# Embedding bags, counted and gathered: 19 features counted and 13 gathered for 20 and 12, with a half round of row buffers behind GpSimd's loop

## What is computed

```python
emb = flat[ids + offs]                                   # (512, 32, 20, 64)
mask = (jnp.arange(L_) < lengths[..., None]).astype(emb.dtype)
pooled = jnp.einsum('bfle,bfl->bfe', emb, mask)
out = pooled.reshape(Bq, F_ * E_)                        # (512, 2048)
return jnp.nan_to_num(out)
```

## Time and profile before

| | |
|---|---|
| median of 3 runs | 1046.8 us |
| the profiled execution | 1047.35 us |
| its span, first to last instruction | 1045.4 us |
| TensorE matmul busy | 983.3 us, 94% |
| TensorE weight load busy | 864.1 us, 83% |
| VectorE busy | 937.4 us, 90% |
| ScalarE busy | 754.1 us, 72% |
| GpSimd busy | 666.0 us, 64% |
| mean share of the 16 DMA engines | about 40% |
| TensorE's granted clock, mean | 0.997 |

### The profile page before, as it was taken

The page is one execution under the profiler, slowest core; times in us unless marked ns, Lnnn a source line. Parts: engine busy times, 40 slices in busy tenths (PEclk is TensorE's granted clock), DMA queues, the critical chain, the costliest instruction groups (busy, mean ns, idle before and its releaser), DMA issues.

```text
span 1045.4 us, 29010 instructions
## 1 busy us (share of the span) xinstructions
PE 983.3 (94%) x9885; PEld 864.1 (83%) x9885; DVE 937.4 (90%) x2485; ACT 754.1 (72%) x1121; POOL 666.0 (64%) x617
## 2 busy tenths in 40 slices
PE   3499999999999999999999999999999999999996
PEld 0188888888888888888888888888888888888885
DVE  9987879898999989999989998999999898999980
ACT  2477777878686868787777777787868686877770
POOL 3874677676676756777667767767676775773010
PEclk9999999999999999999999999999999999999998
DMA  6234142534444343535252626244443434241300
GB/s 220 82 136 118 37 141 67 152 111 131 128 120 135 115 141 105 161 86 179 69 171 76 188 59 191 75 148 119 129 133 115 146 106 116 76 115 50 106 28 6
DMA packets 66140, 119.85 MB, mean 115 GB/s; under 512 B 31600, under 2 KB 33351, under 8 KB 66065
## 3 DMA queue, kind: packets, MB, share of 16 engines
q1 hardware_dynamic: 45696, 100.66, 30.0%
q0 software_dynamic: 19168, 17.93, 8.5%
q10 hardware_dynamic: 1200, 0.58, 0.2%
HBM read 83.45 MB, written 4.71 MB: 84 GB/s over the span
## 4 chain that ended last, share of the span: by engine, by line
PE 79%; DVE 16%; ACT 2%; issue 1%; DVEq 1%; POOL 0%; POOLq 0%
PE sums L530 55%; PE pairs L520 18%; PE rest L548 6%; DVE onehot_j L746 5%; DVE gathered L804 3%; DVE onehot_p L744 2%; ACT table L487 1%; DVE table L755 1%; DVE table L763 1%; ACT counts L475 1%; DVEq L800 1%; DVE is_nan L772 0%; DVE gathered L775 0%; DVE counts L636 0%; DVE j_of L688 0%
## 5 line engine op out<-in xcount | busy, mean ns | idle before, releaser
L530 PE MATMUL sums<-table,counts 128*128 128x192 bf16 x7840 | 806.7, 247 | 0.0
L475 ACT ACTIVATE counts<-pairs 128x588 int16<-128x588 f32 (+1 forms) x880 | 563.7, 651 | 239.5 <-PE pairs L520 232.8
L530 PEld LDWEIGHTS sums<-table,counts 128*128 128x128 fp8e3 x7840 | 690.1, 96 | 44.4 <-issue 0.2
L432 POOL DMA_INDIRECT rows<-tables,row_now x495 | 553.3, 1118 | 245.6 <-PE pairs L520 128.9
L746 DVE TENSOR_SCALAR onehot_j<-ramp,j_of,worth 128x296 bf16<-128x296 f16 x1680 | 491.9, 355 | 0.0
L520 PE MATMUL pairs<-onehot_j,onehot_p 128*128 128x294 bf16 x1720 | 364.6, 292 | 40.6 <-DVE onehot_j L746 28.3
L520 PEld LDWEIGHTS pairs<-onehot_j,onehot_p 128*128 128x128 bf16 x1720 | 159.5, 97 | 101.0 <-issue 27.9
L744 DVE TENSOR_TENSOR onehot_p<-ramp,p_of 128x768 bf16<-128x768 f16 x280 | 153.7, 549 | 72.7 <-PE pairs L520 71.9
L804 DVE TENSOR_REDUCE gathered<-rows 128x64 f32<-128x1280 f32 x48 | 114.3, 2381 | 3.5 <-issue 3.5
L442 POOL DMA_INDIRECT out_gathered<-gathered,place_now x48 | 52.4, 1091 | 69.3 <-issue 67.1
L548 PE MATMUL rest<-table,minus_eye 128*128 128x448 bf16 x320 | 91.5, 367 | 3.6 <-ACT rest L483 1.6
(11 more groups left out here) (67 smaller groups left out, 83.3 us busy)
## 6 DMA issues: line engine op xcount, KB each, us to landing
table<-tables SPq DMA_DIRECT2D x140, 448.0 KB
rows<-zeros SPq DMA_DIRECT2D x48, 640.0 KB
rows<-tables,row_now POOLq DMA_INDIRECT x495
out_counted<-pooled SPq DMA_DIRECT2D x120, 21.0 KB
rows<-lookup_ids SPq DMA_DIRECT2D x1, 817.0 KB, 8.2
rows<-lookup_lengths SPq DMA_DIRECT2D x1, 817.0 KB, 9.7
sorted_records<-records,rank POOLq DMA_INDIRECT x48
out_gathered<-gathered,place_now POOLq DMA_INDIRECT x48
```

The source lines that it names most:

```text
L432: nc.gpsimd.indirect_dma_start(out=rows[:, k, l * E:(l + 1) * E], out_offset=None, in_=table_rows, in_offset=bass.IndirectOffsetOnAxis(ap= ...
L475: nc.scalar.activation(dst, src, ACT.Copy).then_inc(counts_saved, 1)
L530: last = nc.tensor.matmul(sums[h][:, k * PARTS * E:(k + 1) * PARTS * E], counts[h][:, j, :, k], parts[:, :, j, :, 1], start=(j == 0 and k ...
```

## The change

One feature goes from the counted to the gathered ones: M is 19, G is 13, and there are 52 tiles. 52 is six rounds of 8 and a half round of 4, which GpSimd now issues behind its loop (`body(BODIES - 1, False, LAST_BODY)`), with the second put of the last full round and the one put of the half round behind it. The arrays with a column for each tile in rounds have 56 columns, of which four are unused. Tile t is added in stage 41 + 13t // 3. The gathers begin at eviction 45, take 109 evictions for a round, 27 for a pair of tiles and 6/5 for each.

```diff
-M = 20
+M = 19
-FIRST_ADD = 41
-ADD_EVERY = 5
-FIRST_GATHER = 72
-PAIR_OF_TILES = 31
-PER_BODY = 125
+FIRST_GATHER = 45
+PAIR_OF_TILES = 27
+PER_BODY = 109
+
+def add_stage(t):
+    return 41 + 13 * t // 3
 
 def since(l):
-    return 7 * l // 5
+    return 6 * l // 5
...
-    BODIES = TILES // BUFFERS
+    BODIES = -(-TILES // BUFFERS)
+    COLUMNS = BODIES * BUFFERS
+    LAST_BODY = TILES - (BODIES - 1) * BUFFERS
...
-    added_at = {divmod(FIRST_ADD + ADD_EVERY * t, STAGES): t for t in range(TILES)}
+    added_at = {divmod(add_stage(t), STAGES): t for t in range(TILES)}
...
-            def body(b, first):
-                for k in range(BUFFERS):
+            def body(b, first, tiles=BUFFERS):
+                for k in range(tiles):
                     if not first and k % SLOTS == PUT_AT:
                         put(b - 1, k // SLOTS)
                     gather(b, k)
 
             body(0, True)
-            with pool.Fori(1, BODIES) as b:
+            with pool.Fori(1, BODIES - 1) as b:
                 body(b, False)
+            body(BODIES - 1, False, LAST_BODY)
+            for x in range(LAST_BODY // SLOTS, 2):
+                put(BODIES - 2, x)
+            for x in range(LAST_BODY // SLOTS):
+                put(BODIES - 1, x)
             for x in range(2):
-                put(BODIES - 1, x)
-                pool.wait_ge(gathered_stored[x], 16 * SLOTS * BODIES)
+                pool.wait_ge(gathered_stored[x], 16 * SLOTS * (BODIES - 1 + (x < LAST_BODY // SLOTS)))
...
-                fits = has[:, 0:TILES * L].rearrange("p (t l) -> p t l", l=L)
+                fits = has_room[:, 0:COLUMNS * L].rearrange("p (t l) -> p t l", l=L)
...
-                nc.vector.tensor_scalar(later[:], depth_f, -1.4, PAIR_OF_TILES - 2.0, ALU.mult, ALU.add)
+                nc.vector.tensor_scalar(later[:], depth_f, -1.2, PAIR_OF_TILES - 2.0, ALU.mult, ALU.add)
```

More of the change, by code:

```diff
@@ L110, in build_embedding_bag @@
     LAST_WORDS = LAST_BAGS // 2
-    BODIES = TILES // BUFFERS
+    BODIES = -(-TILES // BUFFERS)
+    COLUMNS = BODIES * BUFFERS
+    LAST_BODY = TILES - (BODIES - 1) * BUFFERS
     STAGES = 2 * CHUNKS
-    assert TILES % BUFFERS == 0 and BUFFERS % 2 == 0 and BODIES > 1
+    assert LAST_BODY in (SLOTS, BUFFERS) and BUFFERS % 2 == 0 and BODIES > 1
     assert J % CHUNKS == 0 and GROUPS * GROUP >= HALF and PER_CHUNK % 2 == 0 and CHUNKS * PER_CHUNK == LAST
@@ L123, in build_embedding_bag @@
     STORES = 2 * TRIO + LAST_WORDS
-    added_at = {divmod(FIRST_ADD + ADD_EVERY * t, STAGES): t for t in range(TILES)}
-    assert FIRST_ADD + ADD_EVERY * (TILES - 1) < M * STAGES
+    added_at = {divmod(add_stage(t), STAGES): t for t in range(TILES)}
+    assert add_stage(TILES - 1) < M * STAGES
     LEFT = TILES
@@ L165, in build_embedding_bag @@
         rank = sb("rank", [P, TILES], I32)
-        depth = sb("depth", [P, TILES], I32)
-        later = sb("later", [P, TILES], I32)
-        arrival = sb("arrival", [P, 2, TILES], I32)
+        depth = sb("depth", [P, COLUMNS], I32)
+        later = sb("later", [P, COLUMNS], I32)
+        arrival = sb("arrival", [P, 2, COLUMNS], I32)
         is_nan = sb("is_nan", [P, max(BLOCKS, SLOTS) * E], U8)
@@ L196, in build_embedding_bag @@
         value = piece(L + 1)
-        last_rank = piece(TILES)
+        last_rank = piece(COLUMNS)
         length = piece(TILES, F32)
-        has = piece((L + 1) * TILES, F32)
+        has_room = piece(max((L + 1) * TILES, L * COLUMNS), F32)
+        has = has_room[:, 0:(L + 1) * TILES]
         until = piece((L + 1) * TILES, F32)
@@ L203, in build_embedding_bag @@
         below = piece(L + 1, F32)
-        rank_f, depth_f = piece(TILES, F32), piece(TILES, F32)
-        runs_f = until[:, 4 * TILES:(4 + L // 4) * TILES].rearrange("p (t q) -> p t q", t=TILES)
-        turn_f, arrival_f = (until[:, 2 * x * TILES:2 * (x + 1) * TILES].rearrange("p (x t) -> p x t", x=2) for x in range(2))
+        rank_f, depth_f = piece(TILES, F32), piece(COLUMNS, F32)
+        runs_f = until[:, 4 * COLUMNS:(4 + L // 4) * COLUMNS].rearrange("p (t q) -> p t q", t=COLUMNS)
+        turn_f, arrival_f = (until[:, 2 * x * COLUMNS:2 * (x + 1) * COLUMNS].rearrange("p (x t) -> p x t", x=2)
+                             for x in range(2))
         halves = piece(P + L + 1).bitcast(F16)
@@ L655, in find_depths @@
             def find_depths():
[L657 to L659 removed]
+                fits = has_room[:, 0:COLUMNS * L].rearrange("p (t l) -> p t l", l=L)
+                step(nc.vector.tensor_tensor(fits, below[:, 1:L + 1].unsqueeze(1).to_broadcast([P, COLUMNS, L]),
+                                             last_rank.unsqueeze(2).to_broadcast([P, COLUMNS, L]), ALU.is_le))
                 step(nc.vector.tensor_reduce(out=depth_f, in_=fits, axis=AX_X, op=ALU.add))
```

## The result

| | before | after |
|---|---|---|
| median | 1046.82 us (4 runs) | 1003.6 us (1003.35 to 1004.28, 4 runs) |
| the profiled execution | 1047.35 us | 1004.28 us |
| its span | 1045.4 us | 1002.2 us |
| VectorE's share | 90% | 90% |
| GpSimd's share | 64% | 72% |

The ratio is 0.9587, with a 95% interval of 0.9575 to 0.9599: 4.1% faster. The forecast was 1002.1 us.

A forecast was written before the change was run, and what follows sets the result against it. TensorE was taken to set the pace, VectorE following with 6% of slack. Span 1045.4 - 48.96 + 1.0 + 3.2 = 1000.6, plus 1.95 outside the span, less 0.55 to the median: 1002.1 us, range 999.5 to 1013.

The forecast's parts named there:

- One feature, -48.96 us: TensorE's loop: one counted feature less saves one undisturbed period, 48.96 us.
- Preparation, +1.0 us: Before about 50 us: larger arrays lengthen VectorE's operations on lengths, depths and records, all on the longest chain, +1.0 us.
- Denser adds, +3.2 us: VectorE in the features: 52 adds for 48 cluster with heavy stages and make TensorE wait more, +3.2 us.
- GpSimd, nothing on the path: GpSimd's gathers and puts: asked for 5% too much, yet in time for every add, costing nothing.
- The price of a DMA: GpSimd's mean time for each gather or put, gap included: 1.421 us needed, 1.436 allowed.
- the 30 us that the text gave to FIRST_GATHER: Gathers allowed from eviction 45 instead of 72: 30 us earlier, less preparation, so a first gather at 102.8.
- tile 44's add: VectorE's add in stage 231, the latest to wait for a put of the round before, forecast at 846.4 us.
- The margin: Time by which GpSimd's put (4, 1), 516 DMAs in, is early for the add of tile 44: 7 us.
- Rival 1: GpSimd late: a DMA costs above 1.436 us, so adds wait; 1006 to 1040 us, chance 0.20.
- The last put of all: The last full round's put, moved behind the loop: only the end waits for it, costed at nothing.
- Contention: SBUF port: table cuts hold gathers; the reverse, gathers slowing onehots, was part of rival 2, 1006 to 1011 us, chance 0.08.
- the eleven clusters: Gaps on TensorE in features 3, 7 to 13 and 16 to 18, where VectorE's heavy stages meet: 10.9 us, scaled 11.7.

The follow-up runs named there:

- short adds: Each add reads only its tile's first two rows instead of twenty: 989.91 us against the changed kernel, 1037.56 us against the kernel before.
- light stages: Changed kernel with adds moved at most three stages, off VectorE's table cuts and cleanings, and puts behind one tile's gathers instead of two: 990.18 us.

## Why the prediction was right

**One feature, -48.96 us.** Right: 48.95 measured for an undisturbed feature after, and 48.98 as the mean of all features in both kernels with short adds.

**Preparation, +1.0 us.** Too small: feature 1 begins 1.84 us later. The start varies from run to run: with the same preparation it came at 80.1 to 80.3 in three other kernels and at 78.94 in the one with short adds. The rows of which the term was made grew by 1.4 us together. The operations on 1092 elements did grow by 7% to 8%, but for one. Groups of DVE in the first 53 us, beside the earlier trace rows:

```profile
L645 DVE TENSOR_TENSOR_SCAN counts<-counts 128x1092 f32<-128x1092 f32 x1 | 2.4, 2435 | 0.0
L660 DVE TENSOR_REDUCE counts<-counts 128x52 f32<-128x1092 f32 x1 | 2.4, 2409 | 0.0
...
L669 DVE TENSOR_REDUCE counts<-counts 128x56 f32<-128x1120 f32 x1 | 1.3, 1319 | 0.0
```

L660 was L651 with 1839 ns: +0.57 us alone, where the term had 0.15.

**Denser adds, +3.2 us.** The mechanism was right, the size low by a fifth to a third: +4.0 by the periods, +4.6 by the kernels with short adds. TensorE's waits for onehots came to 11.3 us for the 11.7 foreseen; the features that last longer than 48.96 us are the foreseen ones (3, 7 to 13, 16 to 18) and feature 5 with 0.6 us, and the largest gap is 1.69 us in feature 13, stage 11, for 1.8. But the sum of such waits, on which the term was scaled, is not what the gaps cost. Of the 11.3 us, 0.3 stand ahead of feature 1, 0.9 in feature 18, and three of 0.5 are the turn of a feature, which the 48.96 us hold already. That leaves 8.6 us, where the seventeen periods exceed 48.96 by 12.8; before, 5.8 and 8.8. Scaled on what the gaps cost before, 8.8 + 0.9 = 9.7 us with the last feature's, in place of 8.5, the same model gives 9.7 x 3.0 / 7.9 = +3.7. VectorE's slack fell from 71.9 to 59.1 us, with a feature less, and did not run out.

**GpSimd, nothing on the path.** Right, by less than was thought, and for a reason that was partly wrong. The price of a DMA was exact: from the first gather at 108.0 to the put's end at 841.2, 516 DMAs took 733.2 us, 1.421 each. The start was not: 108.0 for 102.8. Timeline of POOL, beside the earlier trace rows:

```profile
93.55 0.96 POOL L412 DMA_INDIRECT sorted_records<-records,rank  x1 [0.30 <-issue]
99.12 4.48 POOL L418 DMA_DIRECT2D row_now<-sorted_records  x8 [4.61 <-DMA sorted_records<-records,rank]
108.01 1.07 POOL L437 DMA_INDIRECT rows<-tables,row_now  x1 [4.41 <-PE pairs L529]
```

The last scatter was issued at 93.55, 1.8 us later than foreseen, and both landings took 4.4 to 4.6 us, where the estimate had 2.85 for each. So the first gather went out no earlier than before (108.3): of the 30 us that the text gave to FIRST_GATHER none reached it, and the lead over the kernel before comes from round 1 on, begun at 231.0 for 248.6, because nothing paces GpSimd any more. Against that, tile 44's add came at 848.8 for the 846.4 of the estimate. The margin was 3 to 5 us for the 7 foreseen, and the limit (848.8 - 2.5 - 108.0) / 516 = 1.431 us a DMA for 1.436. Rival 1 was near: 16 gathers more, 3% of GpSimd's work, and the time is 1021. That GpSimd stayed inside its slack with a start 5.2 us late owes something to luck: the add came 2.4 us later than foreseen, by TensorE's later start and larger gaps. The last put of all, moved behind the loop and costed at nothing, ended at 971.1, 31 us before the span's end.

**Contention.** Gathers run back to back did not slow onehot_j, and their own mean stayed, though GpSimd now pauses nowhere. Both figures stayed within 0.6%. That cuts hold gathers is borne out: in the trace of after the 87 gathers that began inside a cut took 1.46 us in the mean, the 35 that were running when a cut began 1.28, the others 1.04. The reverse does not show. The cuts that began while GpSimd was at a DMA took 1.08 (L764) and 1.03 us (L772), those that no DMA overlapped 1.08 and 1.05. By the rule of the Trainium skill that was quoted (SBUF — State Buffer, "Who interferes with whom"), the port goes to the one that starts first; for gathers that start first these rows differ, as it is still the gather that gets longer, and the measurement decides.

**What was missed.** The text had the eleven clusters with their places, and took them as the price of the change. They were a choice: the same 52 adds in other stages leave TensorE 1.0 us of such waits. The kernel with its adds in light stages, 990.2 us, has a ratio of 0.9455 to the one before, and is 1.3% faster than the changed one. Likewise GpSimd's price was carried over from the kernel before as if it belonged to the DMA; it moved by 1.7%, to 1102 ns a gather, with the place of VectorE's adds.

## What to carry to other kernels

Where an engine that follows has a small lead and some slack in the mean, look at where its heavy pieces stand before counting how heavy they are. Here 13 us lay between two orders of the same work. Take what a gap costs from the length of the periods and not from the sum of the waits alone. When an engine off the path is asked for more than it can do, count its operations up to the thing that someone waits for, divide the time until then by that number, and compare it with the price of one; the tightest here was not the data but a small write queued behind other tiles' loads. An earlier due time is worth something only if what comes before it is ready.

## What the runs showed of the hardware

- On VectorE, a reduction to 52 sums of 21 elements each, 52 words apart, took 2409 ns, 2.21 ns an element; to 48 sums, 48 words apart, 1839, 1.82 an element; and one that reads 1120 elements in order took 1319, 1.18 an element. Why 52 is so much dearer than 48 was not tried.
- A gather that fetches nothing, all its rows beyond the bound, costs GpSimd as much as a full one: 23.0 us for 16, and the mean of all gathers was 1122 ns with them and 1121 without.
- The price of a gather on GpSimd depends on what runs beside it on VectorE: 1.46 us where it begins inside a table cut, 1.28 where a cut begins during it, 1.04 elsewhere. The mean was 1121 ns in the changed kernel and 1102 with the same work in another order. A cut beside a gather was no longer than one without.
- On some chips the kernel before took 22% longer (1278 us). The traces of the variants run there show ScalarE and VectorE idle for something "remote", up to 30 us at a time; what it is was not found out.
